# Attention of the second layer: one head group in upper and lower parts, the other in fp32, and maxima as one more row of the score product

## What is computed

```python
q = (Q @ w_q.T).reshape(B, S, G, HG, HD)        # 16, 128, 8, 4, 8
k = (K @ w_k.T).reshape(B, S, G, HD)
v = (V @ w_v.T).reshape(B, S, G, HD)
scores = jnp.einsum('bnghd,bmgd->bnghm', q, k) / scale
scores = jnp.where(pad, NEG_INF, scores)
scores = jnp.where(causal, scores, NEG_INF)
attn = jax.nn.softmax(scores, axis=-1)
out = jnp.einsum('bnghm,bmgd->bnghd', attn, v).reshape(B, S, D)
return out @ w_o.T + b_o
```

## Time and profile before

| what | value |
|---|---|
| median of 3 runs | 1570.17 us (1569.85 to 1573.63) |
| profiled execution, own time | 1573.67 us |
| its span, first to last instruction | 1571.9 us |
| mean granted TensorE clock | 0.947 of full speed |
| busy: PE / DVE / ACT / POOL | 1380.7 / 1233.5 / 1019.1 / 776.6 us |
| attention 1, first to last exponential | 1160.8 to 1411.8 us |

### The profile page before, as it was taken

One profiled execution on the slowest core, in us unless ns is written; L12 is line 12 of the kernel. 1 busy time (PEld: TensorE's weight loads), 2 busy tenths in 40 slices (PEclk: granted clock), 3 DMA queues, 4 the chain that ended last, 5 costly groups with the idle time before them and its releaser, 6 DMA issues. The chain is left out here.

```text
span 1571.9 us, 30371 instructions
## 1 busy us (share of the span) xinstructions
PE 1380.7 (88%) x11712; PEld 1184.2 (75%) x11712; DVE 1233.5 (78%) x2446; ACT 1019.1 (65%) x2168; POOL 776.6 (49%) x784
## 2 busy tenths in 40 slices
PE   0367999999999999999999996999769898894995
PEld 0366899999999999999999985677536565563995
DVE  7999888889888888898888896533348978886554
ACT  4688777877777778777777764312146565662773
POOL 2688656566666565666664453101124433341673
PEclk9889999999999999999999997999879998995997
DMA  3100000000100000001010002350252002003563
GB/s 102 37 25 28 15 21 15 27 9 15 35 15 15 21 15 20 16 15 35 15 50 3 2 1 90 70 57 21 58 111 61 14 1 68 1 15 133 182 216 127
DMA packets 62239, 69.85 MB, mean 44 GB/s; under 512 B 5424, under 2 KB 54800, under 8 KB 61968
## 3 DMA queue, kind: packets, MB, share of 16 engines
q1 hardware_dynamic: 59488, 60.54, 14.4%
q0 software_dynamic: 2432, 7.34, 1.4%
q10 hardware_dynamic: 176, 0.04, 0.0%
HBM read 55.56 MB, written 12.34 MB: 43 GB/s over the span
## 5 line engine op out<-in xcount | busy, mean ns | idle before, releaser
L904 POOL TENSOR_TENSOR RB<-YS,M 128x512 bf16<-128x512 f32 x128 | 161.5, 1262 | 243.8 <-DVE YS L759 243.8
L579 ACT ACTIVATE QT<-B,sm 128x256 f32<-128x256 f32 x256 | 130.7, 562 | 164.6 <-PE B L435 164.6
L455 PE MATMUL SS<-QT,KT 128*128 128x256 f32 x512 | 154.9, 397 | 10.5 <-DVE mx L714 10.3
L1768 POOL TENSOR_SCALAR_AFFINE_SELECT P<-P 128x1024 f32<-128x1024 f32 x64 | 81.8, 1277 | 154.2 <-ACT P L1622 154.2
L900 POOL TENSOR_TENSOR yy<-vv,half 128x12 f32<-128x12 f32 x64 | 147.4, 2303 | 5.3
L403 PE MATMUL PA<-WH,XQ 128*128 128x256 f32 x512 | 141.3, 307 | 6.0 <-ACT SQ L608 6.0
L405 PE MATMUL PA<-WL,XQ 128*128 128x256 f32 x512 | 129.9, 285 | 0.0
L733 DVE TENSOR_TENSOR QN<-QN,yy 128x512 f32<-128x512 f32 x128 | 125.3, 979 | 3.1 <-POOL yy L900 3.1
L726 DVE TENSOR_REDUCE vv<-SQ 128x6 f32<-128x768 f32 x128 | 120.6, 942 | 0.3 <-ACT SQ L611 0.3
L714 DVE TENSOR_REDUCE mx<-SS 128x4 bf16<-128x512 f32 x128 | 88.0, 687 | 40.1 <-PE SS L447 39.3
L435 PE MATMUL B<-identf,QN 128*128 128x128 f32 x768 | 106.1, 275 | 5.4 <-ACT LNT L534 5.4
(11 more groups left out here) (331 smaller groups left out, 4502.6 us busy)
## 6 DMA issues: line engine op xcount, KB each, us to landing
W<-in_w SPq DMA_DIRECT2D x16, 1024.0 KB, 7.9
Q<-qsc SPq DMA_DIRECT2D x48, 128.0 KB
WR<-in_wprojT SPq DMA_DIRECT2D x16, 256.0 KB, 2.9
K<-ksc SPq DMA_DIRECT2D x12, 256.0 KB
qsc<-T POOLq DMA_DIRECT2D x8, 384.0 KB, 4.2
X<-in_x SPq DMA_DIRECT2D x4, 512.0 KB, 5.8
CR<-in_xctxT SPq DMA_DIRECT2D x8, 256.0 KB, 2.7
RSM<-rsm_d SPq DMA_DIRECT2D x16, 128.0 KB, 4.1
```

Of the source, the lines that this page charges most:

```text
L455: pe.matmul(SS[:, 256 * z:256 * z + 256], k[:, 128 * z:128 * z + 128], q[:, 256 * z:256 * z + 256], start=True, stop=False)
L579: a.activation(QT[i % 2][:, o:o + 256], B1[:, o:o + 256], ACT.Identity, bias=col(n + "b"), scale=col(n + "w"))
L904: p.tensor_tensor(RB[i % 2][:], YS[:], M[:], ALU.subtract).then_inc(s_rb, 1)
```

## The change

- **Values.** `VS` keeps plain fp32 values (9 columns for each group), which ScalarE writes straight from PSUM. The copy through `VR`, GpSimd's copy and VectorE's subtraction go. Per block GpSimd makes `VPH` (upper part) and `VPL` (lower part) of the even groups and `VPF` (fp32) of the odd ones: three instructions for one.
- **Weighing.** Only the even group's 512 columns are split (`act_upper`, `dve_lower` at half size); its products are upper x upper, lower x upper, upper x lower. The odd group is one fp32 product of 512 columns. `P1` gets a third buffer, and the exponential waits for the weighing three steps back.
- **Maxima.** `K6` gets a row of ones (partitions 48 and 112), `Q6` a row for the negated maxima. Maxima of a block of four steps are collected in `mxb` (32 columns), turned by one product with the negative identity (`pe_max_turn`), copied to `MT` by ScalarE (`act_max_turned`), and put into `Q6` by two DMAs of 16 pieces of 256 bytes that SP issues (`sp_maxima`), all at n = 4b + 5. `pe_shifted_1` has four products of 49 rows, and waits for these DMAs once a block. In SP's program `sp_maxima` stands in the loop behind the 48 loads of `Q6`.
- **Order.** The lag of shifted, exponential and select goes from 2 to 7, and all that follows by 5 as well. The loop has 79 indices for 78; `NEXT` moves by 5; n = 40 stays.
- **Normalise** works from PSUM in two operations instead of four. **Bias** goes to GpSimd (`pool_bias`, at n = 4b + 6), ahead of the residual.

```diff
@@ SP
+        def sp_maxima(sp, b):
+            sp.wait_ge(s_mte, b + 1)
+            for half in range(2):
+                sp.dma_start(Q6[64 * half + 48:64 * half + 49, :, 128 * b:128 * b + 128],
+                             MT[b % 2][16 * half:16 * half + 16, :]).then_inc(s_mr[b % 2], 16)
...
-            for n in range(N1 + 14):
+            for n in range(N1 + 15):
+                b = every(n, 4, 5, NB)
+                if b is not None:
+                    sp_maxima(sp, b)
@@ TensorE
+        def pe_max_turn(pe, b):
+            pe.wait_ge(s_mx, N + 4 * b + 4)
+            if b:
+                pe.wait_ge(s_mte, b)
+            if b >= 2:
+                pe.wait_ge(s_y0, N + 2 * b - 3)
+            if b >= 3:
+                pe.wait_ge(s_oe, b - 2)
+            pe.matmul(SS[0:32, 256:384], mxb[b % 2][:], negib[:], start=True, stop=True).then_inc(s_mt, 1)
@@ def pe_shifted_1
-            pe.wait_ge(s_mx, N + i + 1)
+            if i % 4 == 0:
+                pe.wait_ge(s_mr[b % 2], 32 * (b // 2 + 1))
...
-            for n in range(8):
-                pe.matmul(STB[:, 128 * n:128 * n + 128], mx1[i % 2][:, n:n + 1].broadcast_to([128, 128]), negib[:],
-                          start=n % 4 == 0, stop=False)
...
-                r = slice(64 * half, 64 * half + 8 * NP)
+                r = slice(64 * half, 64 * half + 8 * NP + 1)
@@ def pe_weigh_1
-                pe.matmul(ps_[:], vp[:, o:o + 128], PH1[i % 2][:, :, n], start=g % 4 == 0, stop=False)
-                t = pe.matmul(ps_[:], vp[:, o:o + 128], PL1[i % 2][:, :, n], start=False, stop=g % 4 == 3)
...
+            pe.matmul(OT[u % 2][:], vh[:, o:o + 128], PH1[i % 2][:], start=i % 2 == 0, stop=False)
+            pe.matmul(OT[u % 2][:], vl[:, o:o + 128], PH1[i % 2][:], start=False, stop=False)
+            pe.matmul(OT[u % 2][:], vh[:, o:o + 128], PL1[i % 2][:], start=False, stop=False)
+            t = pe.matmul(OT[u % 2][:], vf[:, o - 32:o + 96], p1, start=False, stop=i % 2 == 1)
@@ pe_attention_1
-                if 0 <= n - 2 < N1:
-                    pe_shifted_1(pe, n - 2)
-                if 0 <= n - 4 < N1:
-                    pe_weigh_1(pe, n - 4)
+                b = every(n, 4, 5, NB)
+                if b is not None:
+                    pe_max_turn(pe, b)
+                if 0 <= n - 7 < N1:
+                    pe_shifted_1(pe, n - 7)
+                if 0 <= n - 9 < N1:
+                    pe_weigh_1(pe, n - 9)
@@ ScalarE
+        def act_max_turned(a, b):
+            a.wait_ge(s_mt, b + 1)
+            if b >= 2:
+                a.wait_ge(s_mr[b % 2], 32 * (b // 2))
+            a.activation(MT[b % 2][:], SS[0:32, 256:384], ACT.Copy).then_inc(s_mte, 1)
...
-            if i >= 2:
-                a.wait_ge(s_lo, i - 1)
-            a.activation(P1[i % 2][:], STB, ACT.Exp, bias=mcf[:, b:b + 1], scale=SC1).then_inc(s_ex, 1)
+            if i >= 3:
+                a.wait_ge(s_LO, N + i - 2)
+            a.activation(P1[i % 3][:], STB, ACT.Exp, bias=mcf[:, b:b + 1], scale=SC1).then_inc(s_ex, 1)
@@ GpSimd
+            even, odd = VS[:, b, ::2, :], VS[:, b, 1::2, :]
+            p.tensor_copy(VPH[b % 2][:, 1:5, 0:9], even).then_inc(s_vp, 1)
+            p.tensor_copy(VPF[b % 2][:, 1:5, 0:9], odd).then_inc(s_vp, 1)
+            p.wait_ge(s_vp, 3 * b + 2)
+            p.tensor_tensor(VPL[b % 2][:, 1:5, 0:9], even, VPH[b % 2][:, 1:5, 0:9], ALU.subtract).then_inc(s_vp, 1)
+
+        def pool_bias(p, b):
+            if b == 0:
+                p.wait_ge(s_mask, 1)
+            p.tensor_tensor(X[:, b, :], X[:, b, :], BO[:], ALU.add).then_inc(s_xb, 1)
@@ sp_feed_forward_0
+            sp.wait_ge(s_vone, 2)
             for half in range(2):
+                sp.dma_start(K6[64 * half + 48:64 * half + 49, :, :].rearrange("o g (b t) -> o (g b) t", t=128),
+                             ones1[:]).then_inc(s_kg, 16)
```

More of the change, by code:

```diff
@@ L1406, in build @@
         WG = sb("WG", [128, 2, E])
-        VP = [sb(f"VP{i}", [128, 9, 128], FR) for i in range(2)]
-        OTS = [sb(f"OTS{i}", [128, 512]) for i in range(2)]
         AO = [sb(f"AO{i}", [128, H]) for i in range(2)]
         AOT = sb("AOT", [128, 2, 128])
-        OS = sb("OS", [128, 4, 4, 9])
         rl = sb("rl", [128, 4, 4])
[L1413 to L1416, removed]
+        VPH, VPL = ([sb(f"VP{n}{i}", [128, 5, 128], FR) for i in range(2)] for n in "HL")
+        VPF = [sb(f"VPF{i}", [128, 5, 128]) for i in range(2)]
+        OTS = [sb(f"OTS{i}", [128, 512]) for i in range(2)]
+        PH1 = [sb(f"PE1{i}", [128, 2, 256], FR) for i in range(2)]
+        PL1 = [sb(f"PL1{i}", [128, 2, 256], FR) for i in range(2)]
+        P1 = [sb(f"P1{i}", [128, 1024]) for i in range(3)]
+        mxb = [sb(f"mxb{i}", [128, 32], BF16) for i in range(2)]
+        MT = [sb(f"MT{i}", [32, 128], BF16) for i in range(2)]
         ti = sb("ti", [128, 128], I32)
@@ L1532, in pe_turn_1 @@
             pe.wait_ge(s_rt, N + u + 1)
[L1533 to L1534 removed]
+            if u % 2 == 0:
+                pe.wait_ge(s_mte, min(b + 2, NB))
+                if b:
+                    pe.wait_ge(s_oe, b)
             if u % 2 and b:
@@ L1646, in act_attention_1 @@
             after_feed_forward_0(a)
-            for n in range(N1 + 14):
-                u = every(n, 2, 6, 2 * NB)
+            for n in range(N1 + 15):
+                b = every(n, 4, 5, NB)
+                if b is not None:
+                    act_max_turned(a, b)
+                u = every(n, 2, 11, 2 * NB)
                 if u is not None:
                     act_evac_out(a, u)
-                b = every(n, 4, 10, NB)
+                b = every(n, 4, 15, NB)
                 if b is not None:
                     act_out_turn(a, b)
[L1654 to L1658, removed]
+                if 0 <= n - 8 < N1:
+                    act_upper(a, n - 8)
+                if 0 <= n - 7 < N1:
+                    act_expo_1(a, n - 7)
+                b = every(n, 4, 33, NB - 4)
                 if b is not None:
@@ L1727, in dve_attention_1 @@
             after_feed_forward_0(v)
[L1728 to L1729 removed]
+            for vp in VPH + VPL + VPF:
+                t = v.tensor_scalar(vp[:].rearrange("p g n -> p (g n)"), identf[:, 0:1].broadcast_to([128, 640]), 0.0, None,
                                     ALU.mult)
             t.then_inc(s_vpz, 1)
[L1732 removed]
+            for n in range(N1 + 15):
                 if n == 40:
                     dve_routing_constants(v)
[L1735 removed]
+                b = every(n, 4, 34, NB - 4)
                 if b is not None:
                     dve_logits(v, b)
[L1738 removed]
+                u = every(n, 2, 12, 2 * NB)
                 if u is not None:
                     dve_normalise(v, u)
[L1741 to L1743 removed]
+                if 0 <= n - 8 < N1:
+                    dve_lower(v, n - 8)
+                b = every(n, 4, 16, NB)
                 if b is not None:
@@ L1783, in pool_attention_1 @@
             after_feed_forward_0(p)
-            for n in range(N1 + 14):
+            for n in range(N1 + 15):
                 if n == 40:
                     pool_routing_constants(p)
-                b = every(n, 4, 0, NB)
+                b = every(n, 4, 4, NB)
                 if b is not None:
                     pool_values(p, b)
-                if 0 <= n - 2 < N1:
-                    pool_select(p, n - 2)
+                b = every(n, 4, 6, NB)
+                if b is not None:
+                    pool_bias(p, b)
+                if 0 <= n - 7 < N1:
+                    pool_select(p, n - 7)
                 if n in NEXT and NEXT[n] <= 2:
@@ L1825, in build @@
         who = (B2[:, 0:3 * E], PC[:, 0:3 * E])
-        s_slots, s_sub, s_exp, s_oh, s_A, s_who, s_idx, s_wgt = (
-            sem(n) for n in ("slots", "sub", "exp", "oh", "A", "who", "idx", "wgt"))
+        s_slots, s_sub, s_exp, s_oh, s_A, s_who, s_idx, s_wgt, s_hi = (
+            sem(n) for n in ("slots", "sub", "exp", "oh", "A", "who", "idx", "wgt", "hi"))
         s_e = [sem("e0"), sem("e1")]
```

133 lines of the change are left out of this document (56 added, 77 removed).

## The result

The changed kernel took 1588.1 us as the median of six runs (1581.4 to 1614.6), against 1570.0 for the kernel before in the same rounds: ratio 1.0089, 95% interval 1.0059 to 1.0119. Ratios here are over fast executions alone (the one of 1614.6 is left out) and are not the quotient of the medians. That the two sets differ so much is itself part of the answer.

What follows compares the result with a forecast made beforehand. TensorE, 13.25 us of a 13.69 us block, bounds the loop, with the exp-select-copy ring within 0.5 us. 1570.2 + 41.5 + 2 + 11 + 6 - 3 - 1.7 - 0.4 = 1625.6 us; range 1597 to 1648.

Steps and rivals of the forecast that it cites:

- The start: Before attention 1's loop: the first products wait for maxima DMAs issued behind all 48 Q6 loads; first exponential +41.5 us.
- its own sign of being wrong: Forecast wrong if the first exponential comes before 1190, or a steady block takes under 13.7 us.
- the forecast 1200.4: Time at which block 0's maxima land in Q6, queued behind the loads.
- the loop's term of +14: Attention 1's loop: steady blocks +11 us, late blocks +6, bursts -3.
- The +2 for the clock at the restart: Loop start: TensorE restarts at the lower clock after standing idle; +2 us (0 to 7).
- The bound of -4 for the landing: Range's allowance for the first maxima landing earlier, near 1196 by SP's program order alone: 4 us less.
- Behind the queue or past it: Forecast: maxima land behind the Q6 loads. Rival: they pass the queue, first exponential about +13, total 1597 us, chance 0.06.
- Blocks: Attention 1's four-step blocks: TensorE-bound, 14.4 us against 13.69, +0.7 each for 16, +11 us.
- Late blocks: Blocks from about step 28 that also carry next_turn and logits: 16.5 us against 15.12, +6 us for ten.
- The two waits: Late blocks: logits wait for ScalarE's copy of z, the turn for VectorE's copy of the logits; together 0.8 us.
- Ring-bound and faster rivals: Loop: the ring's saving comes through, 1582 us, chance 0.1; or the lead removes bursts and late waits, 1551, chance 0.03.
- Late maxima in each block: Rival, attention 1's loop: each DMA pair lands 2 us after shifted is ready, 32 us in all, 1657 us, chance 0.08.

Runs made afterwards that it cites:

- the two sets: The changed kernel timed twice with nothing altered, each with its own profile: 1588.1 us (ratio 1.0089), then 1605.9 us (ratio 1.0191).
- the first experiment: Changed kernel with 36 of the 48 Q6 loads issued in parts of six behind the maxima's DMA pairs of blocks 0 to 5: 1575.1 us, ratio 1.0020.
- weighing alone: Kernel before with the new values, weighing, normalising and bias, but old maxima subtraction, lag of 2 and no maxima DMAs: 1593.7 us, ratio 1.0143.
- 18 columns: Changed kernel with loads between the maxima, even groups' upper and lower values side by side, two products for three: 1564.0 us, ratio 0.9949.
- maxima alone: Kernel before with only the maxima as a 49th row, their transfers and the lag of 7: 1622.0 us, ratio 1.0326.
- the product's removal: Changed kernel with the odd group's fp32 product replaced by one more fp32r product, odd values left out: 1564.0 us, ratio 0.9960.

## Why the forecast had the sign and missed the size

**The start.** Right in its mechanism: SP's program order and the data ahead of the maxima hold shifted(0), and the first experiment takes just that away. The term of +41.5 us was mis-sized: it measured +14.6 in the first profile and +44.3 in the second of the same kernel. The step that failed is that the end of the loads near 1199 was read from one execution and taken as a constant. The first exponential came 27.0 us ahead of the forecast 1202.3. Of these, 18.0 are that the loads took 47.2 us of issue instead of 65.2. Another 7.6 are that they began at 1119.3 instead of 1126.9: 2.3 us from attention 0, 3.0 from the last `pe_down` (7.66 us in the chain at a granted clock of 0.78, where the kernel before had 10.70 at 0.55), the rest from feed-forward 0 between them. The last 1.4 are a shorter way from the last issue to the exponential. The beginning varies as well: in the profiles of the changed kernel and its variants it lies between 1119.3 and 1125.7, so the change need not be its cause. The prediction named its own sign of being wrong, a first exponential before 1190, and 1175.3 is that. In the second profile the maxima landed at 1203.0 for the forecast 1200.4: that this set came out inside the range is the length of the loads in these executions, and part luck, for the loop's term of +14 was wrong in both. The +2 for the clock at the restart can't be told apart in these rows (0.50 until 1180). In the kernel before this length costs nothing, since only the first quarter is waited for; the change puts all of it in the path. The bound of -4 for the landing should have been some -27.

**Behind the queue or past it.** By the Trainium skill (DMA: Bandwidth & Descriptors, Queues, rings and completion order) each engine takes the descriptors of one ring in order, so the maxima stand behind the loads on every ring that both use. The runs agree: the chains have 6.0 and 11.2 us for the first pair of the two profiles, where the median landing of all 32 was 1.7, and the landing comes when the traffic ends. In the first profile the maxima landed at 1173.3, and the DMA share was 0.25 from 1171 to 1172 and 0.05 in the next microsecond. In the first experiment the second and third pair, issued while six loads were still moving, took up to 5.4 and 4.5 us, which no engine waited for.

**Blocks.** In early blocks TensorE is the bound, as summed: 41.90 of 41.90 us, and the sums from rows, 15.8 (weighing alone) and 14.04 (the change), met 15.76 and 13.95. The 13.05 for 18 columns, which is the measured 13.95 less four times 0.23, met 13.04. What I added on top, 0.2 for odd ends and 0.2 because "the bound is never met exactly", was wrong; a queue with nothing to wait for met it exactly. The steady ones among the early blocks cost +0.26 to +0.30 each, not +0.7.

**What the loop gave back.** Forecast +14, measured -0.7 and -3.6. Block by block, the -0.7 of the first profile is made of five parts. The two first blocks give -1.32 (12.26 and 13.37 against 13.47 and 13.48), the next three +0.85. The three with root rounds give -5.43, the other six late ones +8.47, and the end -3.29. At the end no raw scores are left: the block of steps 56 to 60 takes 13.51 against 15.18 and the last three intervals 9.10 against 10.72. I noted that TensorE does raw(0) to raw(6) while it waits, and priced it at nothing because they are done once. But in a TensorE-bound loop work done early is saved, and it comes back there: 3.3 us against the kernel before, of at most 7 x 0.87 = 6.1. The gain of the first blocks is not of this kind. They do their raw scores as all others do, but the weighing starts two steps later. The windows of the fp32 product alone (L1541: busy us of PE and PEld, clock, DMA share, GB/s) have half as many in the first block, and the first 5 us of it are at the lower clock:
```profile
1175.30:1187.60 12.30, 2.93 (x4) 1.04 (x4) 0.67 0.01 2
1187.60:1201.00 13.40, 4.08 (x8) 1.52 (x9) 1.00 0.01 1
```
Of the root rounds, the block with the second fell from 23.79 to 20.11, and the one with the first from 18.35 to 16.85. In the kernel before the routing constants (n = 40) stand beside the second round; with the lag of 7 they fall one block earlier. The two halves bear this out: weighing alone keeps the old lag and takes 24.34 there, maxima alone takes 20.50, and 20.46 in the block ahead of it, where the kernel before has 16.56.

**Late blocks** are dearer than forecast, 17.4 for 16.5 where the clock falls and 15.86 where it does not. The two waits are there as named; that the clock would fall behind them, I had not. In the sum the term still fits, 6 x 1.4 = 8.4 us forecast and 8.47 measured, since these blocks take 15.1 to 16.6 us in the kernel before and not the 15.12 that I started from. Two errors cancel there, which is luck.

**Ring-bound and faster rivals.** The ring came down below 2.9 us a step, as the product's removal shows, but TensorE covers it. Alone, weighing adds 2.1 us a block and maxima buy nothing in one. Maxima alone (ratio 1.0326) is slower than the whole change; weighing alone (1.0143), which has no loads in its path, lies between the whole's two sets (1.0089 and 1.0191) and is slower than the whole with its loads between the maxima (1.0020). Late maxima in each block did not occur: 1.7 us to landing. The one pair behind the 2 MB fill took 7.8, and in the first experiment's profile TensorE waited 1.6 us for it. The score product with its 49th row took 0.32, where I had put 0.40.

## What to carry to other kernels

A small transfer that the first step of a loop needs should not be issued behind a long train of loads that the loop needs only later: the train's length, which cost nothing, becomes part of the path, and so does its variation from run to run. Give it a place between the loads, as needed. When one engine is the bound, sum its work from the distances between starts and add nothing for luck; here that met the blocks in which it never waits, and not the late ones, where it waits and its clock falls. Count what it can do in a forced wait as saved, at the end of the loop, where that work is missing. Before a term rests on the length of a long transfer, look at more than one execution.

## What was not expected of the hardware

The same 48 loads of 128 KB took 47 us of issue in one execution and 60 to 70 in five others, the kernel before and all variants that issue them in one train, at the same DMA busy share (0.55 to 0.56) and with all engines idle beside them both in the execution with 47 us and in the one with 67 (173 and 91 GB/s). Lengths of 60 us and more were seen on two chips (three on one, one on another; that of the kernel before is not on record); why is not settled here. Put between the maxima, the same loads moved 59 to 64 GB/s at that busy share from 1165 to 1200, when nothing waited for them. GpSimd's select had a median of 1.29 us in the kernel before and 1.09 in the changed one:
```profile
L1803 POOL TENSOR_SCALAR_AFFINE_SELECT P<-P x64: 1086/1091/1418, 1176.5 to 1426.8; 128x1024 f32<-128x1024 f32 x64
```
With the old full-size lower copy on VectorE (maxima alone) it was 1.28 again, with the half-size one (weighing alone) 1.09. It goes with the size of that VectorE instruction in these runs, which fell from 1024 columns to 512; the bias is not it, for with the bias back on VectorE the median was 1.09 as well. That instruction was not changed by itself.
